# x added to the attention chunk by chunk on GpSimd, row statistics by chunk, row tiles in pairs, and the output products twelve chunks behind

## What is computed

```python
x = x + autocorrelation(layernorm(x), ctx, ctx)      # 8 heads, along the 512 positions
x = x + ffn(layernorm(x), W, bias, A, Bf, coeffs, scales)

# autocorrelation, for each channel:
corr = ifft(fft(q) * conj(fft(k))).real              # over the positions
w, idx = top_k(corr, 12); w = softmax(w)
out = sum_i w[i] * v[min(idx[i] + pos, 511)]
# ffn:
out = h @ W.T + bias + sum_e coeffs[e]*scales[e] * (h @ A[e].T) @ Bf[e].T
```

## Time and profile before

| | |
|---|---|
| three executions | 2645.93, 2648.44, 2648.89 us |
| span of the profiled execution, first to last instruction | 2644.4 us |
| PE busy | 2497.7 us (94%) |
| DVE busy | 1901.7 us (72%) |
| GpSimd (POOL) busy | 2155.5 us (82%) |
| ScalarE (ACT) busy | 1055.7 us (40%) |
| DMA | 613.19 MB, 550028 packets, 232 GB/s mean |
| mean granted TensorE clock | 0.984 |

### The profile page before, as it was taken

The page is one execution under the profiler, slowest core; times in us unless marked ns, Lnnn a source line. Parts: engine busy times, 40 slices in busy tenths (PEclk is TensorE's granted clock), DMA queues, the critical chain, the costliest instruction groups (busy, mean ns, idle before and its releaser), DMA issues.

```text
span 2644.4 us, 36606 instructions
## 1 busy us (share of the span) xinstructions
PE 2497.7 (94%) x12288; PEld 1559.9 (59%) x12288; DVE 1901.7 (72%) x4966; ACT 1055.7 (40%) x1906; POOL 2155.5 (82%) x1558
## 2 busy tenths in 40 slices
PE   4999866799999999999999999999999999999998
PEld 3655555566666656666666666666666666654444
DVE  5989989778787788777877788778876688645000
ACT  4788855533443343533443334533333233201000
POOL 5799999778998799988998899888998899654222
PEclk8999978899999999999999999999999999999999
DMA  9399998966788687966887687957786687758853
GB/s 325 99 261 269 269 244 198 231 192 209 254 266 228 219 252 238 277 203 210 258 270 210 217 275 248 271 181 236 253 250 172 219 265 243 199 203 301 268 180 114
DMA packets 550028, 613.19 MB, mean 232 GB/s; under 512 B 322640, under 2 KB 448720, under 8 KB 532176
## 3 DMA queue, kind: packets, MB, share of 16 engines
q1 hardware_dynamic: 549840, 610.86, 76.6%
HBM read 383.22 MB, written 151.00 MB: 202 GB/s over the span
## 4 chain that ended last, share of the span: by engine, by line
PE 53%; POOL 22%; DVE 8%; DMA 7%; SPq 5%; issue 4%; ACT 1%; POOLq 0%; DVEq 0%; ACTq 0%
PE f_ps L840 11%; PE f_ps L844 11%; PE f_ps L842 11%; PE a_ps L718 7%; PE a_ps L805 5%; PE a_ps L763 4%; POOL a_zu L1115 4%; POOL f_x1p L1115 4%; POOL a_rows L1115 3%; DMA a_w_lag<-a_w_row 2%; PE a_ps L821 2%; PE a_ps L820 2%; POOL a_zv L1115 2%; POOL a_zf L1115 2%; PE a_ps L768 1%
## 5 line engine op out<-in xcount | busy, mean ns | idle before, releaser
L840 PE MATMUL f_ps<-f_whi,f_hhi 128*128 128x512 f16 x2048 | 777.3, 380 | 5.6 <-issue 2.4
L844 PE MATMUL f_ps<-f_whi,f_hlo 128*128 128x512 f16 x2048 | 777.4, 380 | 0.0
L842 PE MATMUL f_ps<-f_wlo,f_hhi 128*128 128x512 f16 x2048 | 777.4, 380 | 0.0
L924 ACT ACTIVATE a_side<-a_ps 128x256 f32<-128x256 f32 (+1 forms) x320 | 128.0, 416 | 873.5 <-PE a_ps L805 698.4
L844 PEld LDWEIGHTS f_ps<-f_whi,f_hlo 128*128 128x128 f16 x2048 | 200.6, 98 | 242.3 <-issue 1.1
L842 PEld LDWEIGHTS f_ps<-f_wlo,f_hhi 128*128 128x128 f16 x2048 | 200.7, 98 | 230.8 <-issue 1.1
L840 PEld LDWEIGHTS f_ps<-f_whi,f_hhi 128*128 128x128 f16 x2048 | 200.7, 98 | 220.6 <-issue 6.7
L1115 POOL TENSOR_TENSOR a_prod<-a_prod,a_tf 128x512 f32<-128x512 f32 x128 | 160.2, 1273 | 138.7 <-DVE a_tf L1242 138.7
L1115 POOL TENSOR_TENSOR a_zv<-a_zv,a_tw 128x512 f32<-128x512 f32 x128 | 183.3, 1450 | 100.5 <-DVE a_tf L1242 100.5
L805 PE MATMUL a_ps<-inv,a_prod 128*128 128x256 f32 x1024 | 239.5, 388 | 25.6 <-POOL a_prod L1115 25.6
L1115 POOL TENSOR_TENSOR f_x1p<-f_x1p,f_y 128x512 f32<-128x512 f32 x128 | 172.7, 1381 | 101.0 <-DVE f_y L1242 101.0
(11 more groups left out here) (137 smaller groups left out, 5236.6 us busy)
## 6 DMA issues: line engine op xcount, KB each, us to landing
f_whi<-whi_scratch SPq DMA_DIRECT2D x128, 512.0 KB, 5.1
f_wlo<-wlo_scratch SPq DMA_DIRECT2D x128, 512.0 KB, 6.5
a_rows<-in_x_dram SPq DMA_DIRECT2D x62, 1024.0 KB, 8.7
vs<-in_ctx_dram SPq DMA_DIRECT2D x64, 512.0 KB, 6.2
xs<-in_x_dram SPq DMA_DIRECT2D x64, 512.0 KB, 8.0
parts_scratch<-a_so SPq DMA_DIRECT2D x64, 512.0 KB, 7.5
x_scratch<-a_rows SPq DMA_DIRECT2D x32, 1024.0 KB, 5.1
f_x1p<-x_scratch SPq DMA_DIRECT2D x32, 1024.0 KB, 6.8
```

What stands on the lines that cost most here:

```text
L840: nc.tensor.matmul(f_ps[:, t, :], h_hi[q][:, kq, rows_t], w_hi[u % WR][:, :, kq, :], start=(k == 0), stop=False)
L842: nc.tensor.matmul(f_ps[:, t, :], h_hi[q][:, kq, rows_t], w_lo[u % WR][:, :, kq, :], start=False, stop=False)
L844: mm = nc.tensor.matmul(f_ps[:, t, :], h_lo[q][:, kq, rows_t], w_hi[u % WR][:, :, kq, :], start=False, stop=(k == DB - 1))
L924: return nc.scalar.activation(out, source, ACT.Copy, **how)
```

## The change

`LAG` goes from 14 to 12, so there are 76 windows: 0 to 11 attention alone, 12 to 63 both, 64 to 75 products alone. The chunk of x is loaded (`load_addend`) into a buffer `xa`, GpSimd adds it to `so` (`add_rows(w-1)`, near the end of its window `w`), and SyncE stores the sum straight into x1 (`store_x1`). `parts`, `load_attn` and `add_row` go. VectorE takes the statistics of the sum chunk by chunk (`row_statistics(w-2)`, behind `multiply_queries(w)`) and closes them once per sequence (`row_gains`). Row tiles are then loaded from x1 and normalised two per window, in the windows 1 and 2 of each 8, with two buffers each for the float16 halves; the copy of the high half to PSUM for the first four tiles goes. `close_statistics` runs once per sequence on four columns, not once per tile. GpSimd's fold buffer `tq` becomes the buffer `tw`, with a wait on `q_folded` in `multiply_lower`.

```diff
-LAG, KQ, WR = 14, 4, 3
+LAG, KQ, WR = 12, 4, 3
...
+        def row_tiles(w):
+            b, i = divmod(w - CHUNKS - 1, CHUNKS)
+            per = TB // ROW_WINDOWS
+            return range(TB * b + per * i, TB * b + per * (i + 1)) if 0 <= b < BATCH and i < ROW_WINDOWS else range(0)
...
+            def load_row(w, r):
+                at_least(sp, rows_done, stats_before(w))
+                at_least(sp, lo_done, r - 1)
+                sp.wait_ge(pw_summed, OT)
+                sp.wait_ge(x1_out, 16 * CHUNKS * (r // TB + 1))
+                sp.dma_start(rows[r % 2][:, :], x1s[r * T:(r + 1) * T, :]).then_inc(rows_in[r % 2], 16)
+            def load_addend(n):
+                if n >= N:
+                    return
+                at_least(sp, x1_made, n)
+                sp.dma_start(xa[:, :, :], chunk_of(x, n)).then_inc(xa_in, 16)
+            def store_x1(n):
+                sp.wait_ge(x1_made, n + 1)
+                sp.dma_start(sums_of(x1s, n), so[:, :, :]).then_inc(x1_out, 16)
...
                 if 1 <= w <= N:
-                    store_parts(w - 1)
-                if w >= CHUNKS and w % CHUNKS == 0 and w // CHUNKS <= BATCH:
-                    load_attn(TB * (w // CHUNKS - 1), True)
+                    store_x1(w - 1)
+                    load_addend(w)
...
+            def add_rows(n):
+                pool.wait_ge(xa_in, 16 * (n + 1))
+                pool.wait_ge(out_moved, n + 1)
+                add(so[:, :, :], xa[:, :, :], ALU.add).then_inc(x1_made, 1)
...
                 if 1 < w <= PREPARED:
                     tile_low(2 * w - 3)
+                if 1 <= w <= N:
+                    add_rows(w - 1)
...
+            def row_statistics(n):
+                dve.wait_ge(x1_made, n + 1)
+                for k in range(TB):
+                    op = nc.vector.bn_stats(f_bn[:, k, n % CHUNKS, :], so[:, k, :])
                 op.then_inc(bn_done, 1)
...
                 if w < N:
                     multiply_queries(w)
+                if 2 <= w <= N + 1:
+                    row_statistics(w - 2)
+                if low:
+                    row_low(low[0])
...
-                if row_tile(w - 1) is not None:
-                    row_low(w - 1, row_tile(w - 1))
+                for r in low[1:]:
+                    row_low(r)
+                if w % CHUNKS == 1 and row_tiles(w):
+                    row_gains(w // CHUNKS - 1)
...
-                if r is not None:
-                    row_statistics(w, r)
                 if 1 <= w <= N:
                     part_output(w - 1)
-                if r is not None:
-                    row_gain(r)
```

More of the change, by code:

```diff
@@ L482, in load_v, with load_stats_row @@
                 shared.load_v(sp, n)
-            def load_rows(w):
-                m, r = stats_tile(w), row_tile(w)
-                if m is None and r is None:
+            def load_stats_row(w):
+                m = stats_tile(w)
+                if m is None:
                     return
-                at_least(sp, rows_done, sum(stats_tile(i) is not None for i in range(w - 1)))
-                at_least(sp, lo_done, sum(row_tile(i) is not None for i in range(w - 1)))
+                at_least(sp, rows_done, stats_before(w - 1))
+                at_least(sp, lo_done, tiles_before(w))
```

234 lines of the change are left out of this document (96 added, 138 removed).

## The result

The changed kernel takes **2765.9 us** (median of 4 runs, 2763.06 to 2768.37) against 2648.57 us before (median of four), a ratio of 1.0449 (95% interval 1.0433 to 1.0466): 4.5% slower. The forecast was 2668 us, with a range of 2641 to 2692.

The account below looks back on a forecast made before the run. PE was taken to bound the full windows and tail, GpSimd the preparation before them. Terms from -41.3 to +42.9 us summed to +19.5 on a 2644.4 us span, giving 2668 us, range 2641 to 2692.

Parts of the forecast that it names:

- Two windows of products alone: Two windows with products alone go and are issued in windows 12 and 13 instead: -41.3 us.
- term 6: At the end, PE reaches the last sequence's products 41 us earlier, after the last half's store: +2.5 us (0 to +10).
- Windows 3 to 8: GpSimd's sum and VectorE's BN_STATS waiting for it lengthen the loop to 40.7 us; with close_statistics +42.9 us.
- Windows 9 and 10: A shorter GpSimd sum, but row_low ahead of multiply_upper in window 10: 74.4 us against 68.6, +5.8 us.
- Start of the products: From window 11 the halves are stored later and two full windows follow: +16.6 us (+8 to +24).
- term 5: The 51 full windows: VectorE's late choice of lags costs +12 us (0 to +35); lost waits give -23.8.
- The -23.8: In the full windows, PE's waits for transposed weights behind store_x1 and the attention's load go: -23.8 us (-28 to -10).
- Rival B: Full windows: late lags hit three windows per sequence, 2 us each, PE dropping to 1.2 GHz: 2692 us, chance 0.11.
- Rival A: Preparation windows: BN_STATS' wait costs nothing, only GpSimd's 2.3 us do: 2637 us; chance 0.22 with its mild form.
- Rivals C and D: C: DMA bounds the preparation, 2680 us, chance 0.07; D: products start only with window 13, 2683 us, chance 0.05.
- near 512: Sign for the forecast: the first correlate with products comes near 512 us.
- waits of PE above 30 us in the full windows: Sign that would prove the forecast wrong: PE waiting more than 30 us in the windows with attention and products.

Follow-up runs that it names:

- lag14: The changed kernel with LAG = 14 as before and nothing else changed: 2786.8 us.
- stats_late: The changed kernel with row_statistics moved from ahead of the upper products to behind the lower products: 2731.7 us.
- chain_cut: The changed kernel with the inverse roots of row_gains and close_statistics cut to four 128x1 products each, leaving the normalisation out: 2653.5 us.
- port: A kernel of its own: VectorE's small instructions alone and beside GpSimd additions of 128x512; twelve tensor_scalar of 128x4 take 13.6 us beside them.
- mixed_bias: The changed kernel with row_gains ahead of the lower products, close_statistics on GpSimd, and add_bias moved up ahead of add_lower: 2728.9 us.
- pool_combo: The changed kernel with both chains on GpSimd ahead of add_lower, and row_statistics behind the lower products except in windows with row_gains: 2672.2 us.

## Why the prediction was wrong

1. *Two windows of products alone* (-41.3): `lag14` shows 35.3 with what term 6 takes off. The two together are right within 4 us.
2. *Windows 3 to 8* (+42.9): +44.2. A period of 40.7 us was forecast and 40.67 to 40.70 measured in windows 3, 4, 6 and 7, with the wait at BN_STATS (49.5 us in six) where the loop put it. `stats_late` confirms the mechanism. `close_statistics` costs 4.9 in window 5, not 2.9: three of its links stand beside GpSimd's `a_zu`.
3. *Windows 9 and 10* (+5.8): +27.6. Window 10 is right (39.9 for 39.0). For window 9 the 35.4 us counted no `row_gains` at all; it is 56.3, and 40.5 with the chain cut, so 5 us of it have another cause, which stays open.
4. *Start of the products* (+16.6): +9.0, in the bounds. With `lag14` these three windows take 96.7 us: the earlier products cost 16.0, and the rest of the change gives 7.0 back.
5. **The step that failed** is in term 5: "`row_gains` with `close_statistics` by some 4 us in a third", inside "2 us per sequence, six of them, +12 (0 to +35)". Measured over windows 12 to 62 the excess is 94.1 us; with the chains cut, 2.8. It failed twice. The chains were priced by their number of links, as if the 128x4 forms (two SBUF inputs, or a `tensor_scalar` from SBUF to SBUF) cost what the 128x1 one did; beside GpSimd one cost 1.1 to 1.2 us, or 5.5 to 9.5, and moving `row_gains` alone from there gave 57 us back. And the slack of 2 to 3.5 us was thought to cover most of the rest; even with `row_gains` in the quiet place the pairs of windows keep 8.5 us, which go only as `close_statistics` and GpSimd's bias move too. The -23.8 held: the transposes' waits fell to 4.3 us, and `chain_cut` loses 2.8 us in 49 windows. Without this term's 12 us and the 2.9 of `close_statistics` the forecast is +4.6 us, and `chain_cut` measures +4.9. So the other terms are right in sum, but partly by luck: in that run windows 9 and 10 are 6.0 us above their term and windows 11 to 13 are 10.3 below.
6. *The end*: -35.3 against -38.8 with term 1.

The rule that bears on it was in the prediction, beside term 3, from the Trainium skill (GPSIMD Engine Reference, Specifications). It was weighed for `row_low` alone, and in one direction: what GpSimd loses. It was also told for two SBUF inputs only, while the longest stalls (5.5 and 9.5 us) stood on a `tensor_scalar` with one, which waits beside GpSimd as well (`port`: 13.6 for 2.4 us). The mean of 2813 ns hid its spread: the tile's row before reads 2281/2328/5586 ns with both inputs in SBUF and 2278/2278/2280 with one in PSUM. That maximum stood beside a 4.51 us addition of GpSimd: VectorE's instruction itself may be held for 3 us. The new form of the small ones had no row before; a first price above would have been one GpSimd addition each (1.25 us, half of the 2.50 in the earlier trace rows), twelve links of it, 15 us in each of seven windows. In six of them the fifteen instructions were busy 13.0 to 13.1 us, and in window 9 17.0, more than that price.

Rival B named the full windows and the late choice of lags, three windows per sequence with 2 us each, and PE at its 1.2 GHz level behind each. That path is the one that came, lower clock included (14.8 us of PE's time), but in one window per sequence with a wait of up to 13.4 us, which a chain held beside GpSimd made; its 24 us were 82. The transposes that it also gave as a reason did not come late. Rival A's aside, that the change would be neutral with a path of 6.5 us in place of 10.6, doesn't follow from its own sum: +19.5 us over six windows is 3.3 us each, a path of about 7.3. Rivals C and D did not happen: DMA's share fell to 0.81 in windows 3 to 8, and the products did start with window 12 (at 526.4 us, not near 512). Of the signs named as proof of error, "waits of PE above 30 us in the full windows" is the one that came, with 75.1.

What stays open: why `row_low` in `mixed_bias` (asked during the bias addition) and in `pool_combo` missed several ends of additions though it had not asked beside a 1x256 one. In `mixed_bias` it came in at about 776.3 us (its end, 778.58, less its own 2.3: an estimate), where GpSimd made no pause either. That is why each placement had to be run.
